# Linear attention's query pass: the squares of the queries taken by GpSimd from VectorE's copy

## What is computed

```
def softmax_kernel_features(data, proj, is_query):
    data_normalizer = 1.0 / math.sqrt(math.sqrt(d))
    ratio = 1.0 / math.sqrt(proj.shape[0])
    data_dash = jnp.einsum('bhnd,md->bhnm', data_normalizer * data, proj)
    diag_data = jnp.sum(jnp.square(data), axis=-1, keepdims=True) * 0.5 * data_normalizer * data_normalizer
    if is_query:
        stab = jnp.max(data_dash, axis=-1, keepdims=True)
    ...
    return ratio * (jnp.exp(data_dash - diag_data - stab) + EPS)
```

## Time and profile before

| | before |
|---|---|
| median of 3 runs | 2280.19 us (2276.53 to 2281.41) |
| the profiled execution | 2284.59 us |
| its span in the profile | 2282.7 us |
| mean granted TensorE clock | 0.842 |
| TensorE busy | 1844.9 us (81%) |
| VectorE busy | 1344.2 us (59%) |
| ScalarE busy | 1055.9 us (46%) |
| GpSimd busy | 563.8 us (25%) |

### The profile page before, as it was taken

One profiled execution on the slowest core, in us unless ns is written; L12 is line 12 of the kernel. 1 busy time (PEld: TensorE's weight loads), 2 busy tenths in 40 slices (PEclk: granted clock), 3 DMA queues, 4 the chain that ended last, 5 costly groups with the idle time before them and its releaser, 6 DMA issues. The chain is left out here.

```text
span 2282.7 us, 30822 instructions
## 1 busy us (share of the span) xinstructions
PE 1844.9 (81%) x9746; PEld 993.9 (44%) x9746; DVE 1344.2 (59%) x2464; ACT 1055.9 (46%) x1916; POOL 563.8 (25%) x708
## 2 busy tenths in 40 slices
PE   5789889958756447777489977999899993999998
PEld 4645755535324320000122244443134343888887
DVE  6446359946111779999678876999655553222211
ACT  2011322214001659999689964333387870222222
POOL 5000000000212017767200003332014443333333
PEclk9989999958887675555599978997699995999999
DMA  3010110024996005234101008788777634577774
GB/s 89 7 44 28 55 35 22 19 91 182 408 408 265 1 18 180 89 116 134 32 26 32 28 17 124 125 125 126 83 89 108 96 95 144 164 210 202 198 212 104
DMA packets 153120, 258.49 MB, mean 113 GB/s; under 512 B 28560, under 2 KB 124673, under 8 KB 148006
## 3 DMA queue, kind: packets, MB, share of 16 engines
q1 hardware_dynamic: 134822, 239.15, 39.8%
q0 software_dynamic: 18176, 17.80, 4.0%
HBM read 215.16 MB, written 57.51 MB: 119 GB/s over the span
## 5 line engine op out<-in xcount | busy, mean ns | idle before, releaser
L1734 PE MATMUL ps<-arena 128*128 x384 | 198.1, 621 | 82.8 <-ACT ps L1817 62.0
L1817 ACT ACTIVATE ps<-ps,arena 128x512 f32<-128x512 f32 x384 | 256.1, 724 | 9.1 <-POOL arena L1798 9.1
L1744 DVE TENSOR_REDUCE arena<-ps 128x1024 f32 x192 | 232.8, 1224 | 29.0 <-PE ps L1734 18.0
L2186 DVE TENSOR_REDUCE arena<-ps 128x1024 f32 x192 | 221.1, 1213 | 11.9 <-PE ps L2432 9.5
L2655 ACT ACTIVATE arena<-ps 128x1024 f32<-128x1024 f32 x192 | 185.8, 1022 | 90.6 <-PE ps L2533 89.5
L2992 ACT ACTIVATE arena<-ps,arena 128x256 f32<-128x256 f32 x234 | 89.7, 482 | 235.8 <-PE ps L2957 235.7
L2432 PE MATMUL ps<-arena 96*128 96x512 bf16 x500 | 163.6, 432 | 25.0 <-DVE arena L2186 11.5
L1976 ACT ACTIVATE arena<-ps 128x1024 f32<-128x1024 f32 x192 | 178.9, 1043 | 10.6 <-DVE arena L1996 5.2
L2927 POOL DMA_INDIRECT out_dram<-arena x78 | 121.2, 1554 | 238.6 <-DVE arena L3016 168.6
L3012 DVE TENSOR_TENSOR arena<-ps,arena 128x384 f32<-128x384 f32 x39 | 21.8, 558 | 258.7 <-PE ps L2968 258.7
L531 PE MATMUL ps<-arena 96*128 96x456 f32 (+1 forms) x512 | 168.7, 481 | 6.0 <-DMA arena<-la_xt 4.8
(11 more groups left out here) (395 smaller groups left out, 3144.9 us busy)
## 6 DMA issues: line engine op xcount, KB each, us to landing
arena<-in_sm_w_dram SPq DMA_DIRECT2D x128, 576.0 KB, 16.6
arena<-in_re_w_dram SPq DMA_DIRECT2D x39, 1252.0 KB, 5.9
arena<-ra_parts SPq DMA_DIRECT2D x192, 192.0 KB, 9.6
routed_in<-routed_in SPq DMA_DIRECT2D x8, 3332.0 KB, 14.0
ra_parts<-arena SPq DMA_DIRECT2D x48, 192.0 KB, 2.4
arena<-routed_in SPq DMA_DIRECT2D x39, 196.0 KB, 5.4
arena<-la_xt SPq DMA_DIRECT2D x16, 384.0 KB, 3.4
arena<-arena SPq DMA_DIRECT2D x64, 96.0 KB, 2.2
```

The costliest lines, as they stand in the source:

```text
L1734: ins = pe.matmul(ps[:, 2 * (n % 4) + t % 2, :], QM[j][:, h, t * P:(t + 1) * P], KI[:, b, h // HG, :], start=True, stop=True)
L1744: v.tensor_reduce(MXq[:, b, 2 * u:2 * u + 2, at_head(h)], ps[:, 2 * (n % 4):2 * (n % 4) + 2, :], AX.X, ALU.max).then_inc(s_lk, 1)
L1817: ins = act.activation(bank, bank, ACT.Exp, bias=nb[n % 4][:, t % 2:t % 2 + 1], scale=c_reg, accum_out=RS[:, b, t, at_head(h):at_head(h) + 1])
L2186: v.tensor_reduce(MX[:, bass.ds(b, 1), 2 * (n % 2):2 * (n % 2) + 2, n // 2].rearrange("p o t -> p (o t)"), ps[:, 2 * (n % 2):2 * (n % 2) + ...
```

## The change

VectorE's copy of the queries now signals `qk`, and GpSimd, which has a loop of its own in this block, squares the copy in place and signals `qsq`. VectorE takes the maxima in the meantime, without a wait for its own result behind them, then waits for `qsq` and sums the squares. The multiply L820 is gone from VectorE's queue. The number of linked instructions for each tile falls from four to two, and the base of the link's count with it.

```
-    qp, qd, qe, qt, qc = S1("q_products", T, T + 1), S1("q_features", T, 2), S1("q_exp", T, 2), \
-        S1("q_turned", T, 2), S1("q_turned_copied", T, 2)
+    qp, qk, qsq, qd, qe, qt, qc = S1("q_products", T, T + 1), S1("q_copied", T), S1("q_squared", T), \
+        S1("q_features", T, 2), S1("q_exp", T, 2), S1("q_turned", T, 2), S1("q_turned_copied", T, 2)
...
                 qp.wait(v, b, t + 1)
                 q = ps[:, 2 * j, 0:D]
-                v.tensor_copy(SQ[j], q)
-                link(v.tensor_reduce(mq[j].rearrange("p (g h) -> p g h", g=2), features(t), AX.X, ALU.max))
-                link(v.tensor_tensor(SQ[j], SQ[j], q, ALU.mult))
+                v.tensor_copy(SQ[j], q).then_inc(qk.sem, 1)
+                v.tensor_reduce(mq[j].rearrange("p (g h) -> p g h", g=2), features(t), AX.X, ALU.max)
+                qsq.wait(v, b, t + 1)
                 squared_lengths(v, link, t)
...
-                link = Link(v, s_qk, b * (4 * T))
+                link = Link(v, s_qk, b * (2 * T))
...
+
+        @block.gpsimd
+        def _(pool):
+            for s in (qk, qsq):
+                s.start(pool)
+            with pool.Fori(0, B) as b:
+                for t in range(T):
+                    qk.wait(pool, b, t + 1)
+                    pool.tensor_tensor(SQ[t % 2], SQ[t % 2], SQ[t % 2], ALU.mult).then_inc(qsq.sem, 1)
```

## The result

The changed kernel takes 2268.02 us (median of 5 runs, 2260.27 to 2271.05), the kernel before 2280.4 in the same measurement: ratio 0.9939, 95% interval 0.9922 to 0.9957. By the ratio that is 13.9 us less (10 to 18 by its interval), against 5.6 forecast, and outside the stated range. Two later measurements of the same kernel gave 0.9935 (0.9914 to 0.9957) and 0.9945 (0.9924 to 0.9966), so the size is not that of one measurement. The profiled execution took 2268.02 us, its span is 2266.1.

A forecast was written before the change was run, and what follows sets the result against it. VectorE bounds the query pass by a small margin over TensorE. Six steady batches save 4.4 us and the first two 1.1, together 5.6: 2280.19 - 5.6 = 2274.6 us, range 2270.8 to 2279.4.

The forecast's parts named there:

- The cycle with three chains: Query pass, steady batch: three of four per-tile VectorE instruction chains lie on the 19.96 us period; shortened, 19.12.
- d: What one tile's VectorE chain in the query pass gets shorter: 1.39 - 1.11 = 0.28 us.
- the square: GpSimd's 128x192 multiply in the query pass, interpolated at 0.59 us, lower bound 0.46, upper 1.05.
- the trip: From the copy's start through signal, GpSimd's square and signal back until the sum can start: 1.11 us.
- the forecast's case of the shortest square: GpSimd's square at 0.46 us: the maxima set the pace, saving 0.42 us a chain, or up to 0.50.
- the prediction's own conditions: Three bounds on the steady batch period: VectorE's three chains 19.12, mixed VectorE and TensorE path 19.22, TensorE alone 19.1 us.
- Ahead of the steady batches: Batches 0 and 1 of the query pass: two chains' savings, 0.28, and one more chain's, together 1.1 us.
- The tail behind the last chain is unchanged: Query pass after VectorE's last chain: claimed to take as long as before, adding nothing to the 5.6 us.
- a microsecond less here should be one less at the end: Engines meet at the block's end before the soft mixture's loads, so the pass's 5.6 us should reach the total.
- GpSimd at 1.93 times VectorE's time: Rival on the query pass's square: 0.68 us, trip 1.20, gain 4.3 us, 2275.9; chance 0.25.
- The lock: Rival: VectorE's maxima lock GpSimd's square out in the query pass; 1.6 us slower, 2281.8; chance 0.08.
- The slow form: Rival: the query pass's square takes GpSimd's slow 1.05 us; 4.1 us slower, 2284.3; chance 0.09.

The follow-up runs named there:

- two squares: The changed kernel with GpSimd multiplying twice, the first time into a spare tile: 2283.79 us, ratio 1.0004 against the kernel before.

## Why the prediction was wrong

**What bounds the kernel: right.** VectorE was the bound by a small margin. The cycle with three chains gave way to TensorE, and VectorE waits for products 3, where the text had put that wait.

**d was too small.** The failing term is the square: 0.59 us forecast from the 48-wide and the 768-wide row, 0.505 measured. The signal to GpSimd was 0.08 instead of 0.13. The square ends 0.95 us after the start of the copy. With the 0.03 that the way back takes behind the second of two squares, the trip is 0.98 instead of 1.11, and the maxima end at 0.98 too. So d came out at the forecast's case of the shortest square (d = 0.42, maxima set the pace). With d = 0.41 the prediction's own conditions give 19.96 - 1.23 = 18.73, 19.50 - 0.41 = 19.09 and 19.1 for TensorE: 19.1, and 19.12 was measured. Ahead of the steady batches they give 0.82 + 0.28 + 0.41 = 1.5. So 6 x 0.86 + 1.5 = 6.7 us; the traces show 146.6 - 140.2 = 6.4 (means of two and three). This explains 1 us of the 8 that were missed. With 6.4 us the forecast for the median would have been 2273.8, inside the range.

**"The tail behind the last chain is unchanged" failed**, and with it "a microsecond less here should be one less at the end". That was the larger error, and the one that took the result out of the range. It took every row behind the last copy from one execution as a constant. The tail is 2.5 us shorter on the mean of the traces (27.6 against 30.1), though in single ones the order can be turned round. The pass and the tail make 6.4 + 2.5 = 9 of the 13 to 14 us. The remaining 4 to 5, about what an interval reaches to one side, are in the medians but in no column of the traces. The sum by the clock cuts it another way: 9.6 us at the same mean clock, of which the pass is 6.4, and 3 to 4 with the higher clock.

**What is shown and what is not.** Shown: the pass's share; that the square is hidden; that equal work behind the pass takes up to 5 us more or less by the granted clock, in the same kernel and between kernels. Not shown: where the gain beyond pass and tail arises, and why the changed kernel's executions have the higher clock. The moment at which the pass ends was moved on purpose, and 2 to 5 us of the gain may hang on it. How dense TensorE was before it may be another cause; no experiment here separates the two.

**The rivals.** GpSimd at 1.93 times VectorE's time would have been 0.68; it was 0.505, 1.43 times the 0.353. The Trainium skill, "GPSIMD Engine Reference", section "Engine selection", says about twice as slow for two inputs; for this size (VectorE with one input in PSUM) the measurement says less, and it decides. The lock did not come: all 32 squares ran beside the maxima with a mean of 0.505 us and no VectorE wait. This agrees with the Trainium skill, "SBUF — State Buffer", section "Who interferes with whom", by which a reduction on this chip never contends with GpSimd. The slow form did not come either. No rival covered a gain beyond the pass, though the profile had the material: a mean clock of 0.842, and 0.58 in the tail. The range was built of the pass's terms and half the spread of three runs, and was too narrow for that reason.

## What to carry to other kernels

When two engines alternate as the bound, write the cycles down with the number of shortened pieces on each: the formulas gave the period to 0.03 us once the piece was measured. Here an idle engine took an operation at 1.4 times its cost for free, because its trip fitted under something that the first engine had to do anyway; twice the operation did not fit, and the gain was gone. Before taking what lies behind a changed stage as constant, look at the granted clock there. Where it is between its levels, equal work need not take equal time (the tail took 27 to 32 us here), and the range must hold that. And read more than one trace of each kernel, each beside the median of its kernel: a quick execution of the slower one hides the difference.

## What was not expected of the hardware

- The same kernel, unchanged, took from 2271.69 to 2287.89 us in one measurement, in step with the mean granted TensorE clock (0.850 to 0.843).
- GpSimd's 128x192 multiply of a tile with itself takes 0.505 us, while 128x48 took 0.280 and 128x768 took 1.831. A line between these two gives 0.59. Two in a row start 0.46 us apart, less than either lasts.
- At the same mean granted clock (0.847 or 0.848) the changed kernel still takes 9.6 us less than the kernel before, of which the pass explains 6.4.
- Some 9 us of waiting ahead of the dense pass cost the kernel before 2.7 us (ratio 1.0012, 0.9999 to 1.0025), and 6.6 us behind the pass 6.6 (1.0029, 1.0014 to 1.0043). The intervals overlap, so this is a hint only.
